# Flamingo block on one core: the clamp's factor in the norms' constants, means used unnegated, and the key norm's sums begun at D times epsilon

## The reference

```python
x = x + tanh(g_xattn[0]) * L0_xattn(layernorm(x), ctx)   # one head; values are the layer-normed tokens
x = x + tanh(g_ffn[0])   * L0_ffn(layernorm(x))          # quantized feed-forward
x = x + tanh(g_xattn[1]) * L1_xattn(layernorm(x), ctx)   # 16 heads of D = 128
x = x + tanh(g_ffn[1])   * L1_ffn(layernorm(x))          # 64 experts, top 8, and a shared one

def rms_norm(x, g):                        # in L0_ffn, before each of its two linear layers
    return x * rsqrt(mean(x * x) + eps) * g
def activation_quant(x):
    scale = 127.0 / clip(max(abs(x)), 1e-5, None)
    return clip(round(x * scale), -128, 127) / scale
# L1_xattn: q and k are normalised per head over D
q = q * rsqrt(mean(q * q) + eps) * gq;  k = k * rsqrt(mean(k * k) + eps) * gk
scores = (q . k) / sqrt(D);  out = softmax(scores) @ v @ Wo
```

## Time and profile before

| | |
|---|---|
| median of 3 runs | 615.6 us (615.5 to 615.78) |
| profiled execution | 616.09 us, its span 614.3 us |
| busy: PE, PEld, DVE, ACT, POOL | 603.3, 522.6, 477.9, 422.7, 236.7 us |
| TensorE's granted clock | 1.000 of full speed, whole span |
| HBM | 53.45 MB read, 1.31 MB written, mean 89 GB/s |

### The profile page before, as it was taken

One profiled execution on the slowest core, in us unless ns is written; L12 is line 12 of the kernel. 1 busy time (PEld: TensorE's weight loads), 2 busy tenths in 40 slices (PEclk: granted clock), 3 DMA queues, 4 the chain that ended last, 5 costly groups with the idle time before them and its releaser, 6 DMA issues.

```text
span 614.3 us, 11619 instructions
## 1 busy us (share of the span) xinstructions
PE 603.3 (98%) x3644; PEld 522.6 (85%) x3644; DVE 477.9 (78%) x1139; ACT 422.7 (69%) x1082; POOL 236.7 (39%) x282
## 2 busy tenths in 40 slices
PE   8979999999999999999999999999999999999997
PEld 6757899999999999999998888888887888887886
DVE  3999988987777787688876787788777676777776
ACT  6999999888888888889897344465444444443442
POOL 5999998576665566656662020000000000000000
PEclk9999999999999999999999999999999999999999
DMA  8513202000000000000030545453856466545640
GB/s 299 196 53 102 95 11 78 2 2 2 2 2 2 1 2 2 1 2 1 11 121 3 170 147 154 129 171 96 216 156 167 116 176 175 156 154 149 195 128 34
DMA packets 33653, 56.47 MB, mean 92 GB/s; under 512 B 12800, under 2 KB 13504, under 8 KB 33600
## 3 DMA queue, kind: packets, MB, share of 16 engines
q1 hardware_dynamic: 33312, 55.82, 30.4%
q10 hardware_dynamic: 288, 0.00, 0.0%
HBM read 53.45 MB, written 1.31 MB: 89 GB/s over the span
## 4 chain that ended last, share of the span: by engine, by line
PE 89%; DVE 5%; ACT 4%; issue 1%; POOL 1%; DVEq 0%; ACTq 0%; POOLq 0%
PE bank L310 25%; PE bank L312 25%; PE bank L311 25%; PE bank L985 4%; PE bank L960 2%; PE bank L952 2%; DVE hs L2088 1%; PE bank L912 1%; PE bank L1026 1%; PE bank L829 1%; DVE attT_lo L2182 1%; PE bank L835 1%; ACT att L1575 1%; ACT w L1478 1%; PE bank L815 1%
## 5 line engine op out<-in xcount | busy, mean ns | idle before, releaser
L1623 ACT ACTIVATE inter_hi<-inter 128x512 fp32r<-128x512 f32 x63 | 39.8, 632 | 140.5 <-DVE inter L2287 140.5
L310 PE MATMUL bank<-xnT_hi,front_hi 128*128 128x512 f32 (+1 forms) x260 | 102.0, 392 | 0.0
L312 PE MATMUL bank<-xnT_hi,front_lo 128*128 128x512 f32 (+1 forms) x260 | 101.7, 391 | 0.0
L311 PE MATMUL bank<-xnT_lo,front_hi 128*128 128x512 f32 (+1 forms) x260 | 101.6, 391 | 0.0
L2291 DVE TENSOR_TENSOR inter_lo<-inter,inter_hi 128x512 fp32r<-128x512 f32 x63 | 43.6, 692 | 37.9 <-ACT inter_hi L1623 37.3
L1575 ACT ACTIVATE att<-bank,shift,rq 128x256 f32<-128x256 f32 x128 | 71.3, 572 | 0.0
L596 POOL TENSOR_TENSOR att<-att,rowinv 128x512 f32<-128x512 f32 x60 | 63.1, 1067 | 11.1 <-DVE rowinv L2187 11.1
L2260 DVE TENSOR_TENSOR prod<-gate_s,bank 128x512 f32<-128x512 f32 x63 | 43.3, 687 | 21.6 <-PE bank L312 19.5
L2170 DVE TENSOR_REDUCE rowmax<-bank 128x2 f32<-128x512 f32 x64 | 43.6, 686 | 20.7 <-PE bank L312 20.4
L311 PEld LDWEIGHTS bank<-xnT_lo,front_hi 128*128 128x128 f32 x260 | 48.9, 188 | 11.3
L312 PEld LDWEIGHTS bank<-xnT_hi,front_lo 128*128 128x128 f32 x260 | 48.8, 188 | 11.3
(11 more groups left out here) (273 smaller groups left out, 1811.7 us busy)
## 6 DMA issues: line engine op xcount, KB each, us to landing
w_all<-w_rows SPq DMA_DIRECT2D x128, 128.0 KB, 3.0
raw<-in_expert_w SPq DMA_DIRECT2D x32, 384.0 KB, 3.5
wvo_raw<-in_expert_w SPq DMA_DIRECT2D x16, 384.0 KB, 3.5
e_more<-in_expert_w SPq DMA_DIRECT2D x16, 384.0 KB, 3.6
raw<-in_head_qk SPq DMA_DIRECT2D x8, 384.0 KB, 3.1
wvo_raw<-in_head_vo SPq DMA_DIRECT2D x4, 384.0 KB, 3.8
w_keep<-in_head_vo SPq DMA_DIRECT2D x4, 384.0 KB, 3.3
gate_raw<-in_gate_wT SPq DMA_DIRECT2D x2, 704.0 KB, 9.0
```

The costliest lines, as they stand in the source:

```text
L310: pe.matmul(out, l_hi, r_hi_, start=start, stop=False, skip_group_check=True)
L311: pe.matmul(out, l_hi, r_lo_, start=False, stop=False, skip_group_check=True)
L312: return pe.matmul(out, l_lo, r_hi_, start=False, stop=stop, skip_group_check=True)
L1623: act.activation(inter_hi[:, slot, :], inter[:, slot, :], ACT.Copy).then_inc(a_Ihi, 1)
```

## The change

Three things.

1. GAIN leaves the norm weights. The two `scale_gain` instructions are gone, and the roots are taken of smaller numbers instead: in `root_1` the factors become (1 + eps)/GAIN^2 and (eps/GAIN)^2, in `root_2` 1/INTER/GAIN^2 and eps/GAIN^2, so that the power -1/2 brings GAIN back. `times_g1` waits for g1's load, `times_gain` for g2's.
2. `negm` is gone. POOL's `normalise_0` and `normalise_1` subtract the mean from `mv`.
3. The key norm. `mean_k` begins each sum at D * eps, and writes no msq; `rms_k` takes the power of the sums in `ssq` from group 2 on, and waits for the fourth sum. `rk` is so smaller by sqrt(D), and `key_gain` leaves out its factor D^-0.5. `first_mean_k` stays, with the factor 1 and D * eps. At its start `mean_k` now waits for rk of two groups before (g_rk) instead of its own msq (v_mk).

```diff
@@ root_0, root_3
-                pool.tensor_scalar(negm[:, c], mv[:, c, 0], -1.0, 0.0, ALU.mult, ALU.add)
                 pool.tensor_scalar(vare[:, c], mv[:, c, 1], 1.0, EPS, ALU.mult, ALU.add).then_inc(g_va0, 1)
@@ root_1, root_2
-                pool.tensor_scalar(tinyB[:, 0, c], mv[:, c, 1], 1.0 + EPS, EPS * EPS, ALU.mult,
+                pool.tensor_scalar(tinyB[:, 0, c], mv[:, c, 1], (1.0 + EPS) / GAIN ** 2, (EPS / GAIN) ** 2, ALU.mult,
-                pool.tensor_scalar(tinyB[:, 5, c], sumh[:, c], 1.0 / INTER, EPS, ALU.mult, ALU.add).then_inc(g_pw3, 1)
+                pool.tensor_scalar(tinyB[:, 5, c], sumh[:, c], 1.0 / INTER / GAIN ** 2, EPS / GAIN ** 2, ALU.mult, ALU.add).then_inc(g_pw3, 1)
@@ gone, with its two calls (g1 behind normalise_0(5), g2 behind scale_back_1(1))
-            def scale_gain(gain, loaded):
-                pool.wait_ge(loaded, 16)
-                pool.tensor_scalar(gain[:, :], gain[:, :], GAIN, 0.0, ALU.mult, ALU.add).then_inc(g_gain, 1)
@@ normalise_0, normalise_1
-                pool.tensor_scalar(u[:, i, :], x[:, i, :], negm[:, i:i + 1], rstd[:, i:i + 1], ALU.add,
+                pool.tensor_scalar(u[:, i, :], x[:, i, :], mv[:, i, 0:1], rstd[:, i:i + 1], ALU.subtract,
@@ times_gain; times_g1 in the same way with l_g1
-                    pool.wait_ge(g_gain, 2)
+                    pool.wait_ge(l_g2, 16)
@@ rms_k
-                pool.wait_ge(v_mk, n + 1)
+                if n < 2:
+                    pool.wait_ge(v_mk, n + 1)
+                else:
+                    pool.wait_ge(v_sqK, n * 4 - 4)
                 wait(pool, g_kn, n)
-                pool.tensor_tensor(rk[:, :], msq[:, 4:8], minus_half[:, 0:4], ALU.pow).then_inc(g_rk, 1)
+                sums = msq[:, 4:8] if n < 2 else ssq[:, n % 2, 4:8]
+                pool.tensor_tensor(rk[:, :], sums, minus_half[:, 0:4], ALU.pow).then_inc(g_rk, 1)
@@ first_mean_k
-                dve.tensor_scalar(msq[:, 4:8], ssq[:, n % 2, 4:8], 1.0 / D, EPS, ALU.mult, ALU.add).then_inc(v_mk, 1)
+                dve.tensor_scalar(msq[:, 4:8], ssq[:, n % 2, 4:8], 1.0, D * EPS, ALU.mult, ALU.add).then_inc(v_mk, 1)
@@ mean_k
-                wait(dve, v_mk, n - 1)
+                wait(dve, g_rk, n - 1)
...
-                    dve.tensor_tensor_reduce(out=k_sq[:, c // 2, c % 2, :], in0=k, in1=k, scale=1.0, scalar=0.0,
+                    dve.tensor_tensor_reduce(out=k_sq[:, c // 2, c % 2, :], in0=k, in1=k, scale=1.0, scalar=D * EPS,
...
-                wait(dve, g_rk, n)
-                dve.wait_ge(v_sqK, n * 4 - 4)
-                dve.tensor_scalar(msq[:, 4:8], ssq[:, n % 2, 4:8], 1.0 / D, EPS, ALU.mult, ALU.add).then_inc(v_mk, 1)
@@ key_gain
-                dve.tensor_scalar(gk[:, :], gqk_raw[:, 0:1], gqk_raw[:, 1:2], float(D) ** -0.5, ALU.mult,
+                dve.tensor_scalar(gk[:, :], gqk_raw[:, 0:1], gqk_raw[:, 1:2], 1.0, ALU.mult,
```

More of the change, by code:

```diff
@@ L93, in flamingo_kernel @@
         sc2 = sb("sc2", [P, TILES])
-        negm = sb("negm", [P, TILES])
         sumh = sb("sumh", [P, TILES])
@@ L162, in flamingo_kernel @@
         g_va0 = sem("g_va0")
-        g_gain, v_sc1, v_sc2, g_sc1, g_sc2 = (sem(n) for n in ("g_gain", "v_sc1", "v_sc2", "g_sc1", "g_sc2"))
+        v_sc1, v_sc2, g_sc1, g_sc2 = (sem(n) for n in ("v_sc1", "v_sc2", "g_sc1", "g_sc2"))
         g_u0, t_u0, a_x0 = sem("g_u0"), sem("t_u0"), sem("a_x0")
@@ L626, in _ @@
             normalise_0(5)
-            scale_gain(g1, l_g1)
             root_0(3)
@@ L639, in _ @@
             scale_back_1(1)
-            scale_gain(g2, l_g2)
             normalise_0(7)
@@ L2037, in times_g1 @@
                 if i == 0:
-                    dve.wait_ge(g_gain, 1)
+                    dve.wait_ge(l_g1, 16)
                 dve.scalar_tensor_tensor(w1[:, i, :], x[:, i, :], mv[:, i, 0:1], g1[:, :], ALU.subtract,
```

## The result

The changed kernel takes 622.2 us (median; 622.03 to 624.31) against 615.55 us for the kernel before, timed beside it: ratio 1.0113, 95% interval 1.0101 to 1.0126. Forecast were 616.1 us and a range up to 617.1. The prediction was wrong, in size and in where it looked.

A forecast was written before the change was run, and what follows sets the result against it. The prediction took DVE to set the pace from 28.4 to 52.4 us and PE to be full from 57 us. Terms +0.95 - 0.10 - 0.20 - 0.15 = +0.50 us on 615.6 gave 616.1 us, 8-in-10 range 614.7 to 617.1.

The forecast's parts named there:

- negated means of the first norm: Before 28.4 us: dropping four negm and g1's scaling gains nothing, as POOL waits again; 0, bounds 0 and -0.1 us.
- of the third step's norm: Near 54.7 us: without its first negm POOL's u, for which PE waits, comes earlier; -0.10 us, bounds 0 and -0.26.
- u (0.55 us where nothing disturbs it): Near 28.5 us: POOL's u, assumed to keep 0.55 us, runs ahead of the product with g2.
- POOL is in none of these steps.: 28.4 to 52.4 us: the chain of waits runs through DVE alone, so work taken off POOL is not what counts.
- Rival C: Before 53 us: POOL sets the pace, so its removed instructions show, likelier 1.7 us of 2.5; 613.9 us, chance 0.07.
- The hold, +0.95: Near 30 us: POOL's product with g2 starts earlier and holds DVE's rounding L2062; +0.95 us, bounds 0 and +1.02.
- Key norm, -0.35: PE's stalls behind rk near 137 and 319 us shrink by 0.20 and 0.15 us; bounds together 0 and -0.5.
- Rival D: mean_q behind mean_k: POOL's rk holds DVE's msq, 0.86 us per uncovered place; 617.3 or 618.2 us, chance 0.13.
- Signs of being wrong: PE's idle time before 57 us moves by over 1.5 us, or a new PE wait over 0.5 us appears behind it.

The follow-up runs named there:

- e1_gain: Kernel before with the clamp's factor GAIN moved from the norm weights into the roots' constants, alone: 616.84 us, ratio 1.0022.
- e4_gain_key: Changed kernel with the negated means put back, so only the GAIN move and the key norm change remain: 616.25 us, ratio 1.0014.
- e3_key: Kernel before with the key norm change alone: 615.41 us, ratio 0.9995.
- e2_negm: Kernel before with the negm instructions removed and u reading the mean with subtract, alone: 624.42 us, ratio 1.0142.
- e9_first: Kernel before with the new subtract form of u in the first step only: 620.87 us, ratio 1.0082.
- e7_second: Kernel before with the new subtract form of u in the third step only: 618.54 us, ratio 1.0050.
- e8_busy: Changed kernel with 16 instead of 8 filling products on TensorE ahead of the first turn of w: 622.22 us, ratio 1.0114.
- e14_negm_fill: e2_negm with six filling products on TensorE ahead of the third step's first turn of u: 623.56 us, ratio 1.0122.
- e12_order: e4_gain_key with POOL's first product with g2 also made to wait for DVE's fourth rounding of w: 615.51 us, ratio 0.9995.

## Why the prediction was wrong, step by step

- *The failed step.* Under "negated means of the first norm" and "of the third step's norm" the prediction priced the negm instructions that go and nothing else: value 0 and -0.10 us. The instruction that reads the mean instead, with subtract in the place of add, was never priced; "u (0.55 us where nothing disturbs it)" was carried over into the changed kernel. It is 1.23 us, 16 times. Alone this part costs 8.9 us. The trace of before had no subtract on POOL in a tensor_scalar, so the step owed a bound from both sides. That the kind of operation decides on POOL the trace did show: a power of 128x2 takes 0.71 us, a multiply-add of 128x2 0.19, and L532, a max and a multiply of 128x2 with one number per partition, 0.30. No row had 1.23 us, but the change of operation had to stand as an unknown cost on 16 instructions, with a rival of its own.
- *"POOL is in none of these steps."* True of the chain before, and a poor guide to how far POOL was from it. POOL was busy 27.39 of 28.60 us. The prediction also had POOL wait again behind each of the instructions that go. Between 12.51 and 28 us the kernel before shows one such wait:

```profile
23.56 0.49 POOL L487 TENSOR_SCALAR tinyB<-mv 128x2 f32<-128x2 f32 x1 [0.29 <-DVE mv L1980]
```

So POOL had 0.29 us to spare there. Up to 24 us six longer u add 4.0 us (6 x 0.67), four negm and g1's scaling take 1.4 us away (4 x 0.26 and 0.38), and the difference was enough: in the changed kernel DVE waits 2.1 us for POOL's power and PE 2.4 us behind that, and POOL leads the chain from 9 to 23 and from 36 to 60 us. Rival C had the mechanism (POOL counts), with the wrong sign and 0.07.
- *The hold, +0.95.* Right in mechanism: 0.78 us in e1_gain, plus a second hold of 0.43 that the step did not look for and that the kernel before can show as well; by the medians the part costs 1.31 us. In the changed kernel the hold does not arise: POOL is late, its product starts at 32.12 us, behind one rounding (31.27) and 1.5 us ahead of the next (33.65), and both take 0.34 us.
- *Key norm, -0.35.* Right, and a little small: the profile of e3_key shows -0.46, at the two places that were named; the times cannot tell it from nothing. Rival D (rk holds DVE) did not come: DVE's msq for q takes at most 0.49 us in e3_key and 0.47 in the changed kernel, as before, and not the 0.8 that was its sign.
- *The sum without the failed step* was +0.60 (0.95 - 0.35): 616.2 us. e4_gain_key, which is that kernel, took 616.25, 0.72 more than before beside it. That the sum fits so closely is luck in part. By the medians its two terms were each off: 1.31 for the gain part instead of 0.95, and 0.59 less with the key norm instead of 0.35 (616.84 to 616.25), though e3_key alone has 0.12 less.
- *Signs of being wrong.* Both came. The new waits of PE over 0.5 us behind 57 us are there (1.75 and 0.62 us for u), and PE's idle time before 57 us goes from 7.0 to 9.4 us.

## What to carry to other kernels

Price the instruction that stays in a new form as well as the one that goes: the saving of 8 instructions of 0.19 us put 0.67 us on each of 16 others. On GpSimd write "add the negated value", and keep subtract and max off wide tensor_scalars. And before an engine that is not in the chain is called free, compare its slack with the added work up to the next message that somebody waits for, not over the stage.

## What the runs showed of the hardware

- GpSimd's tensor_scalar on 128x256 fp32 takes 0.55 us with add and multiply in either order and 1.22 us as soon as one of its two operations is subtract, or the first is max; per column it is 0.84 ns with add and 3.3 with subtract. With constants in place of numbers per partition it is 0.41 against 1.07. VectorE's same form (L1988, subtract and multiply, 128x256) has no such price: 0.41 us before and 0.39 after at its shortest, where its multiply-and-add of 128x256 (L2062) takes 0.34. GpSimd's tensor_tensor subtracts at the speed at which it adds (0.61 us).
- TensorE's granted clock fell from 1.00 (2.4 GHz) to 0.50 (1.2 GHz) near 28 us in the changed kernel, in e2_negm and in e9_first, where TensorE had been busy 0.8 to 1.0 of the 4 us before, and was back at 1.00 within 6 us. Behind an idle time of 1.7 us near 60 us it fell in e2_negm and not in the changed kernel, e7_second or e8_busy. Where GpSimd set the pace the fall cost nothing (e8_busy), where TensorE did it cost 1.5 us (e2_negm against e14_negm_fill).
- A VectorE tensor_scalar of 128x256 that started inside GpSimd's product of 128x704 took 1.12 us instead of 0.34 and ended 0.14 us behind it (e1_gain); ordered ahead of the product it took 0.34 again (e12_order).
- GpSimd's power of 128x2 took 0.71 to 0.75 us or 1.01 to 1.11 in the same place of the program. It was long in the runs in which it started 0.02 to 0.14 us behind VectorE's tensor_scalar of 128x704, short where it started ahead or 0.01 us behind.
